# Flamingo block on one core: two slots for the stacks of q and k, 18 buffers of exponentials, and one word for the values' products of all sixteen heads of a kind

## The reference, cut to what matters

```
h  = layernorm(x)
y  = softmax(causal(q k^T * scale)) v        # SELF, 16 heads of 8 channels
y += softmax(qc kc^T * scale) vc             # CROSS, keys and values from the context
x  = x + tanh(g0) * (y @ Wp + bp)
h2 = layernorm(x)
combine = route(sigmoid(h2 @ router^T))      # 2 of 4 groups, 4 of 16 experts
x  = x + tanh(g1) * sum_e combine[:, e] * ((silu(h2 @ gate_e^T) * (h2 @ up_e^T)) @ down_e^T)
```

## Time and profile before

| | us |
|---|---|
| median of 3 runs | 332.82 (329.83 to 334.82) |
| the profiled execution | 332.33 |
| its span, first to last instruction | 330.6 |
| TensorE busy | 306.9 (93%) |
| VectorE busy | 263.2 (80%) |
| ScalarE busy | 187.4 (57%) |
| GpSimd busy | 157.3 (48%) |
| mean granted TensorE clock | 0.969 of full |

### The profile page before, as it was taken

How to read it: one execution, slowest core, us unless ns; L and a number is a source line. 1 busy time by engine, 2 the same in 40 slices (tenths; PEclk the granted TensorE clock), 3 DMA queues, 4 the chain that set the end, 5 groups by cost and what they waited for, 6 DMA issues and landing times.

```text
span 330.6 us, 8663 instructions
## 1 busy us (share of the span) xinstructions
PE 306.9 (93%) x3150; PEld 241.0 (73%) x3150; DVE 263.2 (80%) x652; ACT 187.4 (57%) x386; POOL 157.3 (48%) x189
## 2 busy tenths in 40 slices
PE   1759889999999999999999999999999999999896
PEld 1545557776787788778777878878787887787675
DVE  5799878686889899998798898878688885465873
ACT  2240555776887754857456856766566557752220
POOL 6892456473570468034803766077504450441713
PEclk9875979999999999999999999999999999999999
DMA  4363676867637695757645545275354601605012
GB/s 145 92 183 100 208 179 171 225 177 243 157 104 219 147 193 146 193 132 161 182 86 135 134 113 157 72 169 139 96 143 120 120 2 35 129 4 132 16 39 90
DMA packets 37808, 43.71 MB, mean 132 GB/s; under 512 B 4198, under 2 KB 33174, under 8 KB 35478
## 3 DMA queue, kind: packets, MB, share of 16 engines
q1 hardware_dynamic: 36542, 42.57, 51.0%
q10 hardware_dynamic: 1224, 0.59, 0.7%
HBM read 32.59 MB, written 9.18 MB: 126 GB/s over the span
## 4 chain that ended last, share of the span: by engine, by line
PE 76%; DVE 9%; DMA 8%; ACT 2%; issue 2%; SPq 1%; POOL 1%; DVEq 0%; ACTq 0%; POOLq 0%
PE bank L928 15%; PE bank L1010 14%; PE bank L885 9%; PE bank L1046 8%; PE bank L907 8%; PE bank L904 6%; PE bank L882 5%; DMA q_stack<-q_scr 4%; DVE row_max L1115 3%; DMA q_stack<-shiftT 2%; PE bank L943 2%; PE bank L982 2%; DVE k_stack L489 2%; PE bank L934 1%; PE bank L997 1%
## 5 line engine op out<-in xcount | busy, mean ns | idle before, releaser
L1115 DVE TENSOR_REDUCE row_max<-bank 128x2 f32<-128x512 f32 (+1 forms) x224 | 146.6, 685 | 28.0 <-PE bank L885 19.4
L796 ACT ACTIVATE probs<-bank 128x512 f32<-128x512 f32 x224 | 126.0, 596 | 57.2 <-PE bank L904 27.4
L1010 PE MATMUL bank<-xn2T,w_pairs_sb 128*128 128x256 f32 x256 | 66.4, 386 | 1.5 <-DVE f_gate L1195 0.9
L928 PE MATMUL bank<-probs,v_ext 128*32 128x256 f32 (+1 forms) x1024 | 55.8, 359 | 0.1
L885 PE MATMUL bank<-k_stack,q_stack 72*128 72x256 bf16 x256 | 47.1, 283 | 5.2 <-DVE row_max L1115 3.5
L1010 PEld LDWEIGHTS bank<-xn2T,w_pairs_sb 128*128 128x128 f32 x256 | 44.0, 190 | 7.8 <-DVE f_gate L1195 2.4
L708 POOL TENSOR_TENSOR f_h<-f_h,comb 128x512 f32<-128x512 f32 x31 | 38.8, 1268 | 21.9 <-DVE f_h L1203 8.2
L907 PE MATMUL bank<-q_stack,k_stack 73*128 73x256 bf16 x256 | 44.3, 275 | 0.8 <-DMA q_stack<-shiftT 0.3
L928 PEld LDWEIGHTS bank<-probs,v_ext 128*32 128x32 f32 x1024 | 29.6, 110 | 19.6 <-issue 3.6
L882 PE MATMUL bank<-k_stack,q_stack 121*128 121x128 bf16 (+1 forms) x384 | 35.6, 222 | 0.7 <-DVE row_max L1115 0.6
L885 PEld LDWEIGHTS bank<-k_stack,q_stack 72*128 72x128 bf16 x256 | 22.4, 100 | 18.2 <-DVE row_max L1115 9.8
(11 more groups left out here) (126 smaller groups left out, 369.9 us busy)
## 6 DMA issues: line engine op xcount, KB each, us to landing
k_stack<-k_scr SPq DMA_DIRECT2D x45, 192.0 KB
q_stack<-q_scr SPq DMA_DIRECT2D x15, 576.0 KB
comb<-c_scr SPq DMA_DIRECT2D x14, 512.0 KB, 6.6
q_scr<-part SPq DMA_DIRECT2D x45, 64.0 KB
...
```

Of the source, the lines that this page charges most:

```text
L796: nc.scalar.activation(probs[:, seq % NP, :], exp_bank[s % 2][:, :], ACT.Exp).then_inc(exp_done, 1)
L928: last = pe.matmul(pv_bank[32 * n:32 * n + VW, col + q0:col + T], v[:, VW // 2 * odd:VW // 2 * odd + VW], weights, start=odd == 0 and kt = ...
L1010: last = pe.matmul(bank_of[:, n * T:(n + 1) * T], w[:, e0:e0 + 128], xn2T[:, :], start=True, stop=True)
L1115: nc.vector.tensor_reduce(row_max[:, kind, h0:h0 + nh, qt], max_bank[k % 2][:, :].rearrange("p (h k) -> p h k", h=nh), AX.X, ALU.max).then ...
```

## The change

It makes three edits and writes all five lists anew. SLOTS goes from 3 to 2, NP from 10 to 18, and `weigh_values` gets a kind in place of a pair of groups: one word `pv:b:kind` waits for all chunks of exponentials of that kind (16 for CROSS, 12 for SELF, so one CROSS word needs 16 buffers full at once) and runs both halves, each with its own signal on pv_done. The arithmetic is the same. Of the lists PE's has 16 words fewer (pv 32 to 16), and VectorE's two fewer (`tri:0:4` and `tri:0:5`, the third slot's masks); the others hold the same words in another order.

```diff
-SLOTS = 3
+SLOTS = 2
...
-NP = 10
+NP = 18
...
 ORDERS = {
     'pe': '''
         xnT:0 proj:0 vproj:0 proj:0:1 xnT:1 proj:1 proj:1:1 vproj:1 max:0 max:0:1 max:0:2 max:0:3 max:0:4 max:0:5
-        max:0:6 max:0:7 xnT:2 max:0:8 max:0:9 shift:0 proj:2:1 vproj:2 max:0:10 exp:0 max:0:11 exp:0:1 max:0:12 max:0:13
+        max:0:6 max:0:7 xnT:2 max:0:8 max:0:9 shift:0 proj:2:1 max:0:10 max:0:11 proj:2 max:0:12 vproj:2 max:0:13
...
     'dve': '''
-        stats1:0 xnv:0 scale:0 stats1:1 tri:0 sp1:0 stats1:2 sp3:0 tri:0:1 tri:0:2 sp1:0:1 sp3:0:1 tri:0:3 tri:0:4
+        stats1:0 xnv:0 scale:0 stats1:1 sp1:0 sp3:0 tri:0 tri:0:1 stats1:2 sp1:0:1 sp3:0:1 tri:0:2 tri:0:3 tmax:0
...
                         last = pe.matmul(ps[:, n, :], key[0:STACK + 1], q[0:STACK + 1], start=n == 0, stop=n == nh - 1)
                 last.then_inc(exp_scores, 1)
 
-            def weigh_values(b, p):
-
-                kind = (CROSS, SELF)[p // 2]
-                pe.wait_ge(exp_done, b * NC2 + LAST_CHUNK[2 * p + 1] + 1)
-                if p == 0:
+            def weigh_values(b, kind):
+
+                pe.wait_ge(exp_done, b * NC2 + LAST_OF_KIND2[kind])
+                if kind == CROSS:
                     pe.wait_ge(v_ready, b + 1)
-                if p % 2 == 0:
-                    ge(pe, pv_copied, b * 2 + kind)
-                col = p % 2 * T
+                ge(pe, pv_copied, b * 2 + kind)
+                for half in range(2):
+                    weigh_half(b, kind, half).then_inc(pv_done, 2)
+
+            def weigh_half(b, kind, half):
+                col = half * T
                 for odd in range(2):
                     for kt in range(NQ):
                         for n in range(4):
-                            h = first_head(2 * (p % 2) + odd) + 2 * n
+                            h = first_head(2 * half + odd) + 2 * n
                             chunk, h1 = [(c, h1) for c, (kd, k_, h1, nh, q0) in enumerate(S2_CHUNKS)
                                          if kd == kind and k_ == kt and h in range(h1, h1 + 2 * nh, 2)][0]
                             nh, q0 = S2_CHUNKS[chunk][3:]
...
                             v = v_ext[:, b % 2, kind, kt * H // 2 + h // 2].rearrange("p e v -> p (e v)")
                             last = pe.matmul(pv_bank[32 * n:32 * n + VW, col + q0:col + T], v[:, VW // 2 * odd:VW // 2 * odd + VW], weights,
                                              start=odd == 0 and kt == 0, stop=odd == 1 and kt == NQ - 1, tile_position=(0, 32 * n))
-                last.then_inc(pv_done, 2)
+                return last
 
             def transposes(src):
                 for n in range(NQ):
```

More of the change, by code:

```diff
@@ new lines @@
+        max:0:14 exp:0 exp:0:1 xnT:3 max:0:15 max:0:16 shift:0:2 exp:0:2 max:0:17 max:0:18 proj:3 exp:0:3 exp:0:4
+        max:0:19 max:0:20 exp:0:5 max:0:21 exp:0:6 max:0:22 max:0:23 proj:3:1 max:0:24 exp:0:7 exp:0:8 max:0:25 max:0:26
+        exp:0:9 max:0:27 exp:0:10 exp:0:11 shift:0:1 max:1 exp:0:12 max:1:1 exp:0:13 max:1:2 vproj:3 max:1:3 max:1:4
+        exp:0:14 max:1:5 max:1:6 xnT:4 max:1:7 exp:0:15 max:1:8 exp:0:16 exp:0:17 max:1:9 max:1:10 pv:0 max:1:11
+        exp:0:18 exp:0:19 max:1:12 vproj:4 max:1:13 proj:4 max:1:14 max:1:15 max:1:16 exp:0:20 max:1:17 shift:1 exp:0:21
@@ new lines @@
+        max:4:9 ga:1:1 max:4:10 y:2:1 max:4:11 exp:3:17 exp:3:18 max:4:12 pv:3 max:4:13 max:4:14 exp:3:19 ga:1:2
+        exp:3:20 max:4:15 exp:3:21 max:4:16 up:1:1 max:4:17 exp:3:22 max:4:18 yT:2 exp:3:23 max:4:19 exp:3:24 wp:2
+        max:4:20 exp:3:25 up:1:2 max:4:21 exp:3:26 shift:4 exp:3:27 ga:1:3 max:4:22 max:4:23 pv:3:1 exp:4 max:4:24
+        max:4:25 up:1:3 exp:4:1 max:4:26 xn2T:2 max:4:27 exp:4:2 down:1 down:1:1 max:5 logits:2 exp:4:3 down:1:2 max:5:1
+        xnT:6 exp:4:4 down:1:3 down:1:4 exp:4:5 exp:4:6 max:5:2 max:5:3 down:1:5 exp:4:7 down:1:6 exp:4:8 down:1:7 y:3
@@ new lines @@
+        shift:5:1 max:6:1 exp:5:4 exp:5:5 vproj:6 max:6:2 down:2 max:6:3 exp:5:6 xn2T:3 max:6:4 down:2:1 max:6:5
+        logits:3 exp:5:7 exp:5:8 max:6:6 down:2:2 xnT:7 max:6:7 exp:5:9 down:2:3 up:3 exp:5:10 exp:5:11 proj:7 exp:5:12
+        max:6:8 down:2:4 down:2:5 max:6:9 max:6:10 exp:5:13 down:2:6 combT:3 down:2:7 exp:5:14 max:6:11 y:4:1 max:6:12
+        exp:5:15 exp:5:16 max:6:13 ga:3 max:6:14 exp:5:17 max:6:15 pv:5 ga:3:1 proj:7:1 exp:5:18 max:6:16 up:3:1
+        max:6:17 exp:5:19 max:6:18 shift:6 ga:3:2 max:6:19 exp:5:20 yT:4 max:6:20 exp:5:21 up:3:2 max:6:21 max:6:22
@@ new lines @@
+        exp:5:22 exp:5:23 ga:3:3 exp:5:24 max:6:23 wp:4 max:6:24 exp:5:25 exp:5:26 max:6:25 y:5 exp:5:27 up:3:3 max:6:26
+        exp:6 exp:6:1 max:6:27 vproj:7 exp:6:2 exp:6:3 pv:5:1 max:7 exp:6:4 max:7:1 exp:6:5 shift:6:1 down:3 max:7:2
+        exp:6:6 max:7:3 down:3:1 xn2T:4 exp:6:7 max:7:4 down:3:2 logits:4 exp:6:8 max:7:5 max:7:6 down:3:3 exp:6:9
+        exp:6:10 max:7:7 down:3:4 max:7:8 down:3:5 exp:6:11 exp:6:12 down:3:6 down:3:7 exp:6:13 max:7:9 y:5:1 max:7:10
+        exp:6:14 exp:6:15 max:7:11 ga:4 exp:6:16 pv:6 exp:6:17 max:7:12 max:7:13 combT:4 up:4 yT:5 exp:6:18 max:7:14
```

248 lines of the change are left out of this document (113 added, 135 removed).

## The result

The changed kernel took 337.77 us (median of 13 runs, 333.81 to 339.80), the kernel before 333.97 in the same stay (13 runs, 329.83 to 336.46): ratio 1.0123, 95% interval 1.0089 to 1.0157. All ratios take, of each kernel, only the runs within 1.5% of its fastest, so they can differ from the ratio of the medians. The forecast was 326.8 with a range to 331.5. The change made the kernel 1.2% slower where 1.8% faster was forecast, and the time lies 11 us from the forecast. The profiled execution took 338.04, its span 336.3, its mean granted clock 0.959 (before 0.969).

The account below looks back on a forecast made before the run. Bound by VectorE's mask copies before 24 us and everything TensorE issues after 45. Terms -3.5 - 3.0 + 0 + 1.0 = -5.5 took the profiled 332.3 to 326.8 us; 8-in-10 range 322.8 to 331.5.

Parts of the forecast that it names:

- Part 1: Values' products on TensorE: merging 32 words into 16 saves 0.22 us of edge loss each, -3.5 us.
- Halves don't join: Rival: the drain stays between a merged word's two halves, Part 1 gives 0, time 330.3 us; chance 0.05.
- Part 3: Two slots: loads wait for scores of the sequence two before; 0 us, no TensorE wait for q or k over 1 us.
- Part 2: VectorE's chain at the start, until some 45 us: earlier first row maximum, one mask copy fewer, less idling; -3.0 us.
- the sixth copy: Term of Part 2: VectorE's mask copy at 37.23 us, between maxima, is gone; 1.2 us gained.
- the 0.5 of idle time: Term of Part 2: half of VectorE's 0.99 us idle before 33.96, for scores held up by a projection and a vproj.
- The copies block: Rival: GpSimd's clears and normalising slow both pairs of VectorE's mask copies, maxima start at 25.3, time 329.7 us; chance 0.17.
- Part 4: Longer values' words on TensorE delay scores and starve VectorE of row maxima: +1.0 us, bounds 0 and +5.
- ScalarE at 0: Term of Part 4: ScalarE, 57% busy, with 18 buffers running two chunks past a CROSS kind, costs 0 us.
- VectorE becomes the bound: Rival: between 80 and 220 us VectorE becomes the bound, slower than before; middle 338 us; chance 0.08.

Follow-up runs that it names:

- e3: Changed kernel with every merged values' word cut in two again, one word of scores between the halves; ratio to the kernel before 1.0242.
- e1: Kernel before with SLOTS = 2 and without the third slot's two mask copies, lists otherwise as before; ratio to the kernel before 0.9939.
- f4: Kernel before with two slots, without the third slot's mask copies, and 18 buffers, values' words of eight heads as before; ratio to the kernel before 0.9949.
- g3: Changed kernel with GpSimd's first 13 words in the order of before, so its clears of v_ext come later; ratio to the kernel before 1.0048.
- e2: Kernel before with two slots, 18 buffers and merged values' words, each where the second half had stood; ratio to the kernel before 1.0356.
- f1: Changed kernel with row maxima reading half the columns (maxima not the true ones); ratio to the kernel before 1.004.
- f2: Kernel before with row maxima reading half the columns (maxima not the true ones); ratio to the unedited kernel before 0.9944.
- e4: Changed kernel with fhc:1 and fhc:1:1 moved behind the normalising xn2:2 in GpSimd's list, as before; ratio to the kernel before 1.007.
- i1: h2 with ScalarE's exponentials over half of each bank's columns (output not the reference's); ratio to the kernel before 1.0001.
- h2: Changed kernel with the edits of g3 and e4 and comb's load ahead of q_stack's on SP's queue; ratio to the kernel before 1.0000.
- h1: Changed kernel's lists with g3's edit until sequence 1's last score, lists of before until max:6:2, then the changed ones; ratio to the kernel before 1.0195.

## Why the prediction was wrong

- **Part 1 was right.** 3.5 us forecast, 3.2 in the drains after, 4.3 by e3; a CROSS word took 3.59 (3.6 forecast), a SELF word 2.74 (2.75). "Halves don't join" is out.
- **Part 3 was right.** e1 and f4 are 0.5 to 0.6% faster, not slower. The waits of TensorE's weight loads for the stacks between 60 and 160 us were 0.9 and 0.6, under the 1 us that it allowed. The 1.39 us of e1's profile is over it, at the very place that part 3 took for covered; no time was lost by it that the ratio shows.
- **Part 2 failed.** 3.0 us forecast, 0.2 there at 60 us. It priced VectorE up to the first maximum and took TensorE's first scores as bound by the stack loads alone, at 21.32. One pair of copies was slow, as I had taken, and VectorE was free at 22.88 (22.7 forecast); but which pair it was I had left open, and the first also holds `proj`, hence TensorE 2.5 us, which was in no term. So the first scores came at 22.7, and 0.36 us was won at the first maximum instead of 1.0 to 2.0. The other 1.7 us of part 2 (the sixth copy, the 0.5 of idle time) don't show at 60 us either: the sequence's scores started no sooner than its stacks came (40.73 + 6.49), and both profiles spent as much of the stretch from 20 to 60 us at half clock (granted 0.82 in both). "The copies block" named the mechanism and gave 329.7: with one pair, not two. The Trainium skill, SBUF — State Buffer, section "Who interferes with whom", has the instruction issued first block the other. g3 supports that placing GpSimd's work decides (5.0 us against 2.4), but not the order: in the change the copy's record starts at 12.52 and the memset's at 12.55, and the copy took twice its time. Records 0.03 us apart may not show which of the two was issued first.
- **Part 4 failed, in its object more than in its size.** It asked only what stands behind a long word. e2 may show that price (12 us in unfit lists); in the new lists it is not what is paid, since neither faster row maxima (f1 against f2) nor taking the words apart (e3) brought it back. The loss of the new lists was in rows of engines that part 4 didn't cost: GpSimd with `fhc:1` behind a queued load, 1.5 to 1.8 us (e4; 4.9 in the change's profile, with its half clock), the clears (g3, 2.5 us by the ratios), and 4.8 us of short waits between 60 and 160 us. ScalarE at 0 stands (i1).
- **The clock was in no term.** 2.4 us more in the profile.
- **The rival "VectorE becomes the bound" has its 338 by luck.** The time was 337.8, but making VectorE faster (f1, f2) didn't take the difference away, and its place, 80 to 220 us, holds only part of it.

The forecast's sum, -5.5, against the profiles' +5.7: drains +0.3 off the forecast; part 2, 2.8 at 60 us; the middle, 60 to 160 us, 4.8 of waits where 1.0 was forecast, so 3.8; 160 to 180 us, 4.9 (5.7 with its half clock, 0.8 before). These make 11.8; 0.5 less was waited from 180 us on, which leaves 11.3, the 11.2 of difference within the rounding.

**Open:** what the short waits between 60 and 160 us are bound to. They are 8.3 to 8.6 us in all of f1, h2, i1 and the change, whichever engine is made faster, and one releaser takes over from the other. That the old middle would do without them in this kernel wasn't shown, since h1's join spoilt it. They are 3.8 of the 11.2 us that the forecast missed, and what kept h2 at 1.0000.
